# Transformer layer with soft expert slots: buffers lent to the norms in attention's tail, first unit's logits in the norms, last weights ahead of logits

## The reference, cut to what matters

```python
scores = jnp.einsum('bqgsd,bkgd->bgsqk', q, k) * scale
attn = jax.nn.softmax(jnp.where(causal, -jnp.inf, scores), axis=-1)
ctx = jnp.einsum('bgsqk,bkgd->bqgsd', attn, v).reshape(b, n, D_OUT)
x = _layernorm(x + ctx @ Wo + bo)
...
x_ln = (x - mean) / jnp.sqrt(var + LN_EPS) * gamma + beta
x_n, mu_n = _l2norm(x_ln, -1) * scale, _l2norm(mu, 0)
logits = jnp.einsum('bnd,des->bnes', x_n, mu_n)
dispatch = jax.nn.softmax(logits, axis=1)
combine = jax.nn.softmax(logits.reshape(B, N, E * S), axis=-1)
slot_in = jnp.einsum('bnd,bnes->besd', x_ln, dispatch)
h = jax.nn.gelu(jnp.einsum('besd,edh->besh', slot_in, W1) + b1[None, :, None, :], approximate=False)
slot_out = jnp.einsum('besh,ehd->besd', h, W2) + b2[None, :, None, :]
out = jnp.einsum('bsd,bns->bnd', slot_out.reshape(B, E * S, D), combine)
x = _layernorm(x + out)
```

## Time and profile before

| | us |
|---|---|
| median of 3 runs | 2501.87 |
| lowest and highest | 2499.42, 2502.53 |
| the profiled execution's own time | 2493.14 |
| its span | 2491.4 |
| busy in the span: PE, DVE, ACT, POOL | 2406.0, 1734.3, 1428.6, 1610.2 |

### The profile page before, as it was taken

The page is one execution under the profiler, slowest core; times in us unless marked ns, Lnnn a source line. Parts: engine busy times, 40 slices in busy tenths (PEclk is TensorE's granted clock), DMA queues, the critical chain, the costliest instruction groups (busy, mean ns, idle before and its releaser), DMA issues. The chain is left out here.

```text
span 2491.4 us, 38941 instructions
## 1 busy us (share of the span) xinstructions
PE 2406.0 (97%) x12834; PEld 1723.0 (69%) x12834; DVE 1734.3 (70%) x3804; ACT 1428.6 (57%) x2763; POOL 1610.2 (65%) x1751
## 2 busy tenths in 40 slices
PE   8999999999999999998979999999999998999998
PEld 6875455555555555545767888887888886788886
DVE  3378778888888888735876565666656555777776
ACT  3225466666666666664865565666655554454543
POOL 4405677687777777877956767675666775454553
PEclk9999999999999999998989999999999998999999
DMA  7863647474756656465964454566545456664553
GB/s 250 268 197 89 138 106 151 112 148 107 149 112 145 129 130 140 95 132 194 347 188 144 148 154 144 156 209 187 167 130 166 135 161 249 218 209 130 149 153 102
DMA packets 249177, 400.87 MB, mean 161 GB/s; under 512 B 57712, under 2 KB 112016, under 8 KB 237584
## 3 DMA queue, kind: packets, MB, share of 16 engines
q1 hardware_dynamic: 195864, 283.46, 37.2%
q0 software_dynamic: 52480, 114.37, 20.7%
q10 hardware_dynamic: 632, 0.56, 0.1%
HBM read 180.63 MB, written 112.22 MB: 118 GB/s over the span
## 5 line engine op out<-in xcount | busy, mean ns | idle before, releaser
L1155 ACT ACTIVATE p_probs<-p_ps_s 128x512 f32<-128x512 f32 (+3 forms) x1280 | 591.5, 542 | 322.8 <-PE p_ps_s L1073 314.0
L1757 POOL DMA_DIRECT2D p_eT<-p_ex x1024 | 538.4, 535 | 270.3 <-DVE p_ex L2066 218.9
L1182 DVE TENSOR_REDUCE p_parts<-p_ps_m 128x1 f32<-128x512 f32 x752 | 458.7, 680 | 74.7 <-PE p_ps_m L1058 74.5
L1073 PE MATMUL p_ps_s<-q,k_e 98*128 98x512 f32 (+3 forms) x1280 | 468.7, 389 | 3.8 <-ACT p_probs L1155 3.4
L995 POOL TENSOR_TENSOR p_added<-p_added,p_probs 128x2048 f32<-128x2048 f32 x88 | 420.1, 4782 | 31.4 <-ACT p_probs L1155 16.6
L1058 PE MATMUL p_ps_m<-k_m,q 96*128 96x512 f32 (+3 forms) x1232 | 433.5, 386 | 5.5 <-PEq L2360 3.5
L1073 PEld LDWEIGHTS p_ps_s<-q,k_e 98*128 98x128 f32 x1280 | 242.2, 192 | 182.1 <-issue 78.5
L1058 PEld LDWEIGHTS p_ps_m<-k_m,q 96*128 96x128 f32 x1232 | 234.1, 193 | 83.9 <-DVE p_parts L1188 22.2
L1091 PE MATMUL p_ps_c<-p_probs,v_e 128*32 128x512 f32 (+3 forms) x2560 | 284.1, 544 | 6.0 <-POOL p_probs L975 6.0
L1188 DVE CUSTOM_DVE_ANT_0 p_masked<-p_ps_m,p_mask 128x128 f32<-128x128 f32 (+1 forms) x480 | 203.8, 485 | 27.1 <-PE p_ps_m L1058 27.0
L73 PE MATMUL logit_banks<-kept_hi,w_o_lo 128*128 128x512 f32 x512 | 207.9, 406 | 7.1 <-DVE w_o_lo L2013 6.4
(11 more groups left out here) (257 smaller groups left out, 5062.0 us busy)
## 6 DMA issues: line engine op xcount, KB each, us to landing
p_probs<-p_probs POOLq DMA_DIRECT2D x56, 1024.0 KB, 7.5
logits_t<-logit SPq DMA_DIRECT2D x32, 1024.0 KB, 5.0
p_eT<-p_ex POOLq DMA_DIRECT2D x1024, 32.0 KB, 2.0
logit<-logits_t SPq DMA_DIRECT2D x128, 256.0 KB, 3.5
q<-q_t SPq DMA_DIRECT2D x96, 256.0 KB, 4.7
c_first<-L_ffn_W_dram SPq DMA_DIRECT2D x64, 256.0 KB, 5.6
p_probs<-p_probs POOLq DMA_DIRECT2D x16, 768.0 KB, 7.4
p_x<-L_attn_x_dram SPq DMA_DIRECT2D x32, 256.0 KB, 5.0
```

The source lines that it names most:

```text
L1073: pe.matmul(ps_s[:, u % ST_BANKS, q0:BLK], k_e[:, bass.ts(kt, P)], q[:, qb, h, q0:BLK], start=True, stop=True).then_inc(s_score, 1)
L1155: act.activation(probs[s % RING][:, h, q0:BLK], ps_s[:, u % ST_BANKS, q0:BLK], ACT.Exp).then_inc(s_exp, 1)
L1182: dve.tensor_reduce(to, bank, AX.X, ALU.max).then_inc(s_taken, 1)
L1757: pool.dma_start(eT[r][p * QD:(p + 1) * QD, i, :, :], ex[i * QD:(i + 1) * QD, 2 * r:2 * r + 2, bass.ts(p, P)]).then_inc(s_eT[r], 16)
```

## The change

1. **Lent buffers.** Two `spare` buffers of 1 MB (128 x 4 x 512) live through the whole kernel. They serve as two of the input buffers of `projections`, as two of attention's ring of probabilities, as x and context of the norms' first tiles (x of pairs 0 and 1, context of pairs 1 and 2), as `ex` and `most` in the slots, and as rings of `combine`. In attention's tail SP loads the four pieces ahead of the store of block 30 (`next_stage`), ACT and DVE split the context of tiles 0 and 1 into the buffer of the keys `k_m`, and PE multiplies them by Wo (24 matmuls) at the end of its list, into PSUM banks `banks` that attention, norms, slots and combine now share. The norms' loops start with tile 2, and the bias of tiles 0 and 1 follows tile 2's matmuls.
2. **First unit's logits in the norms.** The vectors of unit 0 are loaded in the middle of the norms and split at round 22 into buffers of their own; PE makes the four groups of logits (`first_logits`) between and behind the last transposes. Unit 1's vectors are loaded at round 28 and split at the end. In the slots the parts for these fall away; ACT's first copy waits for the norms' last stores.
3. **Start of the slots.** SP loads two groups of rows, stores unit 0's logits, loads the other two groups and then does the 16 moves of unit 0's half r = 1 itself; POOL does r = 0 only. The splits of row groups 2 and 3 go to the places that they have at the start of the other sequence.
4. **Last weights.** In SP's list the weights, the slots' outputs and the bias of the lag 2 come ahead of `next_logits`.

```diff
+            def next_stage():
+                free(last_use[1])
+                for k in range(2):
+                    sp.dma_start(c_next[k], d["ctx"][0, :, :, bass.ds((k + 1) * 2 * P, 2 * P)].rearrange("g p n -> p g n")).then_inc(s_lent[k], 16)
+                free(last_use[0])
+                for k in range(2):
+                    sp.dma_start(x_first[k], x.rearrange("b n c -> (b n) c")[bass.ds(k * 2 * P, 2 * P), :]
+                                 .rearrange("(t p) c -> p t c", p=P)).then_inc(s_lent[2 + k], 16)
...
                 elif what == "store":
+                    if a == NBK - 2:
+                        next_stage()
                     store(a)
...
+            for n in range(PREPARED):
+                pe.wait_ge(s_clo, n + 1)
+                pe.wait_ge(s_exp, 4 * NS)
+                for g in range(GROUPS):
+                    mm = three_passes(pe, banks[:, n, :], c_hi[n][:, g, :], c_lo[n][:, g, :], w_hi[:, g, :], w_lo[:, g, :], g == 0, False)
+                mm.then_inc(s_proj, 1)
...
+                    if a == NBK - 2:
+                        act.wait_ge(s_cin, 16)
+                        act.wait_ge(s_unit, NU - U0)
+                        for k in range(PREPARED):
+                            act.activation(c_hi[k], c_first[:, :, bass.ts(k, P)], ACT.Copy).then_inc(s_chi, 1)
...
+                    if a == NBK - 2:
+                        for k in range(PREPARED):
+                            dve.wait_ge(s_chi, k + 1)
+                            dve.tensor_tensor(c_lo[k], c_first[:, :, bass.ts(k, P)], c_hi[k], ALU.subtract).then_inc(s_clo, 1)
...
-            load(0)
-            for k in range(1, C3):
-                load(k)
+            load(C3 - 1)
             for i in range(TT + 8):
-                if i == TT:
+                if i == TT // 2:
                     fetch_kept()
+                if i == TT - 4:
+                    sp.wait_ge(s_mlo, 1)
+                    sp.dma_start(kept_mu[:, :, :], mu_e[:, 1, :, :]).then_inc(s_mu, 16)
...
-                if i < TT:
+                if PREPARED <= i < TT:
...
+                    for m in range(PREPARED):
+                        add_bias(m)
+                add_bias(n)
...
+            def first_logits(j):
+                if j == 0:
+                    pe.wait_ge(s_mlo, 1)
+                pe.wait_ge(s_y, TT - JG + j + 1)
+                pe.wait_ge(s_xtlo, (j + 1) * TG)
+                for c in range(DC):
+                    part = bass.ts(c, P)
+                    mm = three_passes(pe, ps_p[:, j, :], m_hi[0][:, c, :], m_lo[0][:, c, :],
+                                      kept_hi[:, j * TG:(j + 1) * TG, part], kept_xT[:, j * TG:(j + 1) * TG, part], c == 0, c == DC - 1)
+                mm.then_inc(s_first, 1)
...
+                if TT <= i < TT + JG - 1:
+                    first_logits(i - TT)
+            first_logits(JG - 1)
...
+            def vectors_hi(n):
+                act.activation(m_hi[n][:, :, :], kept_mu[:, :, :], ACT.Copy).then_inc(s_mhi, 1)
+
...
+                if i == TT - 10:
+                    act.wait_ge(s_kept, 48)
+                    vectors_hi(0)
+                if PREPARED + 2 <= i + 2 < TT:
...
+            act.wait_ge(s_mu, 16)
+            act.wait_ge(s_proj, TT)
+            vectors_hi(1)
...
+            def vectors_lo(n):
+                dve.wait_ge(s_mhi, n + 1)
+                dve.tensor_tensor(m_lo[n][:, :, :], kept_mu[:, :, :], m_hi[n][:, :, :], ALU.subtract).then_inc(s_mlo, 1)
...
+                if i == TT - 10:
+                    vectors_lo(0)
...
-        ex = al.sbuf("p4_ex", [P, JG, BANK])
+        ex, most = spare
         eT = [al.sbuf(f"p4_eT{r}", [P, NQ, 2, P]) for r in range(2)]
-        most = al.sbuf("p4_most", [P, JG, BANK])
...
+        logits_to = lambda count: count - JG
+
+        def moved(n, r):
+
+            if r == 0:
+                return s_eT[r], 256 * (n + 1)
+            return (s_eT[r], 256 * n) if n > 0 else (s_eT_first, 256)
...
+            def first_rows(*groups):
+                def part(n):
+                    if n == 0:
+                        for r in range(R4):
+                            for o in (o_x1, o_xl):
+                                sp.wait_ge(o[r], 16 * TT_ALL // R4)
+                            sp.wait_ge(o_t[r], 16 * NT // R4)
+                        for j in groups:
+                            load_rows(j)(n)
+                return part
...
+            def first_moves(n):
+
+                if n == 0:
+                    sp.wait_ge(s_turn, 4)
+                    for p in range(NQ):
+                        for i in range(NQ):
+                            sp.dma_start(eT[1][p * QD:(p + 1) * QD, i, :, :],
+                                         ex[i * QD:(i + 1) * QD, 2:4, bass.ts(p, P)]).then_inc(s_eT_first, 16)
...
             walk([(0, load_mu)] + [(0, load_unit_rows(j)) for j in range(JG)]
-                 + [(1, first_rows), (1, store_logits)] + [(1, next_logits)]
-                 + [(2, load_weights), (2, next_slots), (2, load_bias), (1, later_rows), (3, later_logits), (3, store_out)])
+                 + [(1, first_rows(0, 1)), (1, store_logits), (1, first_rows(2, 3)), (1, first_moves)] + [(2, load_weights), (2, next_slots), (2, load_bias), (1, next_logits),
+                    (1, later_rows), (3, later_logits), (3, store_out)])
...
-                for r in range(2):
+                for r in range(1 if n == 0 else 2):
...
-                    if j == 0:
-                        pe.wait_ge(s_mulo, n + 1)
+                    if n == 0:
+                        return
+                    if j == 0 and n >= 2:
+                        pe.wait_ge(s_mulo, n - 1)
```

177 lines of the change are left out of this document (106 added, 71 removed).

## The result

Eight runs of each kernel gave a 2493.86 us median for the changed kernel (2491.89 to 2497.14), 2500.34 us for the kernel before (2497.97 to 2502.53). The ratio is 0.9979, with a 95% interval of 0.9969 to 0.9988: 5 us faster (3 to 8). On record stood 2485.4 us, 16.5 us faster. The sign is right and the time lies in the range, but the gain is a third of what was forecast. The profiled execution has a span of 2490.2 us against 2491.4, so the two traces differ by 1.2 us where the medians differ by 6.5.

A forecast was written before the change was run, and what follows sets the result against it. TensorE was taken as busy mid-stage, so gains lie in its waits at stage borders and the last slots unit. 7.7 (attention through slots' start) + 8.8 (last weights) = 16.5 off 2501.87 gives 2485.4 us; range 2476 to 2495.

The forecast's parts named there:

- Attention's end: Attention's end and norms' start: 24 matmuls follow without a gap, 7.3 us of wait removed, norms start 1.7 later, gain 0.9.
- the 0.9: Norms' start: gain taken in us, since POOL starts 1.7 later but has two c_lo fewer, 1.25 each.
- the rule weighed there: Attention's tail: DVE with two SBUF inputs and GpSimd lock a shared port, the second blocked; the add would end 1.4 later.
- 3.0 earlier: Norms' start, best end: two spared c_lo and 5.5 us of PE both count in full against the 1.7.
- Norms' tail: First logits in the norms' tail: slots start 3.0 us later, at 1280.05, with unit 0's logits done and its vectors hidden.
- Slots' start: Start of the slots: unit 2's logits at S'+38.2 against 48.9 before; 7.7 us earlier, all from attention on included.
- the rule on issuing engines: Slots' start: all issuers' transfers share 16 engines, a second issuer saves only issue time, 8.5 us for 16 moves.
- Last weights: Slots' end: weights land earlier, PE's wait on p_si falls from 7.55 to some 0.9; gain 8.8 us, ends 6 and 10.7.
- B: Rival, chance 0.13: the slots' start gives nothing as transfers bind the first products; only last weights count, 9 us; 2492.9.
- C: Rival, chance 0.05: PE's wait at the last unit moves to the first low half or p_siT, 2 of 8.8 left; 2492.2.
- D: Rival, chance 0.04: slower, 16 small moves between row loads bring DMA down at the slots' start; 2508.6 at 120 GB/s.
- A: Rival, chance 0.18: more gain, no queue at the slots' start and clock held at the end, 22.8 us; 2479.1.

The follow-up runs named there:

- f3: The kernel before with only the first part of the change (lent buffers, next stage's loads and 24 matmuls in attention's tail): ratio 1.0000 to the kernel before.
- e3: The changed kernel with the first unit's vectors split at round 19 of the norms instead of 22: ratio 0.9965 to the kernel before.
- e4: The changed kernel with all moves of the first unit issued by GpSimd, none by SP: ratio 0.9968 to the kernel before.
- f2: The changed kernel with vectors split at round 19 and all first-unit moves on GpSimd: ratio 0.9940 to the kernel before, 15.0 us faster.
- e1: The kernel before with only the last part, weights, slot outputs and bias ahead of combine's logits in SP's list: ratio 0.9964, 9 us faster.
- h3: f2 with the 16 loads of low slot outputs issued by SP instead of GpSimd: drain 10.51 us; its kernel time is not given.

## Why the prediction was wrong

By its own steps:

**Attention's end: waits right, gain not there.** The 24 matmuls follow without a gap, and the wait shrinks from 7.3 to 3.5. The norms start 1.9 later against attention's last sums, forecast 1.7. The term that was mis-sized is the 0.9: the two spared c_lo, priced at 1.25 each, bring 2.0 by tile 5, just what the later start costs, and by the slots' start f3 is 0.6 later instead of 0.9 earlier (139.9 us from attention's last sums, 139.3 before). In time it is 0, with 2.5 to either side. The price of the subtracts had the wrong side: the rows were read as lengthening the add by up to 0.6 a subtract, and the rule weighed there as doing so by 1.4; the add, issued first, kept its 4.8, and the subtract took 4.2 to 6.3. Nothing shows that this cost anything, as both were done before PE needed them. The end "3.0 earlier" doesn't follow from its own terms (2.5 + 5.5 - 1.7 is 6.3), and nothing hangs on it.

**Norms' tail: this step failed.** "Its vectors (0.7 on ACT and DVE) come ten tiles earlier and are hidden", and "The one vector subtraction added to DVE in the norms (0.69) is in these ends": the subtraction was priced by its duration at most. It measured 3.9 us: y of tile 31 comes 123.0 us behind the norms' start, 119.2 in f3, which lacks it, and 120.0 with it at round 19 (e3). The prediction had both durations in front of it, 1.25 and 1.83 for c_lo, and used them only for attention's tail; from tile 21 on DVE idles 0.03 a tile (0.5 to 0.7 before), and there the order of the two engines decides which of them pays, and before it was the one that could afford it. The last group of logits was priced at the full clock, 2.8, and took 4.6 at 0.64; e4 has 3.0 behind the same wait, so this was bad luck of the clock and not a wrong price, as far as the traces tell. From attention's last sums to the slots' start it takes 148.2 instead of 139.3: 9.0 later, forecast 3.0 (6.8 by the times from the spans' starts, since attention's sums ended 2.2 earlier in the second trace).

**Slots' start: right.** Unit 2's logits came 39.8 behind the start, forecast 38.2, before 48.9. The idle time ahead of product 0 is 9.8 (forecast 9), though the product came at 23.9 and not at 21, and the work after it ran at half clock. Having SP do the moves was no help (e4), as the rule on issuing engines that the prediction weighed would have it. The gain of the whole start is 9.1 us, and 9.0 of it are spent before the slots begin, where 3.0 were forecast.

**Last weights: right in the unit, wrong at the barrier.** Alone it gave 9.0 against the 8.8 forecast; the clock fell (0.72 between 2080 and 2092) and the last unit was 7.3 shorter. In the whole change only 2 reach the end. No step of the prediction asked which engine arrives last at the barrier once DVE is 6 us earlier, nor what taking 16 DMAs off GpSimd's queue does beyond their issue time. With the old list of DMAs the same gain comes through (f2, e4).

**The sum.** 16.5 was forecast, 5 measured. With the two losses taken out it is 15.0, and part of that closeness is luck: the distances in f2's trace add up to 11.7 (norms' end 4.3 later, start 9.3 and last unit 6.7 shorter). In the changed kernel they add up to 2.4 (9.0 later, 9.1 and 7.3 shorter, 5.0 lost at the barrier), so some 3 us of both measured gains aren't found in the traces, each of a single execution. The rivals named a transfer (B), a wait behind p_si (C) and the DMA queue (D); none of them was it, nor was the sum of A and C. That the times of B and C, 2492.9 and 2492.2, lie next to the measured 2493.86 is luck: B has the start giving nothing, which came true, but by transfers, and C has 2 us left of the last weights, which came true, but by a wait in the unit.

**Open.** In every execution but the profiled one of the kernel before, the start of the second sequence takes 1.3 to 4.6 us longer from unit 17's to unit 18's store (29.9 to 33.2, against 28.5), also in kernels whose program there is that of before (e1 30.3, f3 32.7). So it is no effect of the change; why it varies is open. Open too are what sets the drain, what decides the clock of the last 12 matmuls, and the 3 us above.

## What to carry to other kernels

An instruction added to an engine without idle time costs more than its duration if it shifts that engine against another with which it shares a port: look whether the durations in the steady rounds behind it stay, and put it into rounds that have idle time. Before pricing two such engines side by side, ask which of them is issued second: in every pair shown here, that one paid. Before crediting a gain at the end of a stage, ask for each engine when it reaches the barrier, GpSimd's drain included, since the profile's idle times hide it. A change of several parts can measure a third of their sum: time each alone.

## What was not expected of the hardware

GpSimd's DRAIN at the end of the slots stage took 2.67, 3.98 or 10.51 us by what it had issued on its DMA queue before, each value the same to the nanosecond in single executions of up to eight different kernels, though the last DMA of its own had landed 0.2 us before or, in h3, 17. And two engines kept a phase, 3.63 us a tile with c_lo at 1.83 and xl at 0.74, or 3.95 for seven tiles with c_lo at 1.47 and xl at 1.06, from one instruction of 0.69 us. A DVE subtraction of 0.69 us that began 0.2 us behind a GpSimd add of 4.8 took 6.29.
